# A four-layer graph network on one core: edge counts kept as 16-bit integers and widened on ScalarE

## What is computed

```python
# layer 2
neigh_mean = segment_sum(x[src], dst) / max(deg, 1)
h = x @ W_self.T + neigh_mean @ W_neigh.T + bias
x = layernorm(x + layernorm(h) * gamma + beta)
# layer 3, twice (relu between), r in {0, 1} by edge type
gate = sigmoid(x_j @ gate_w[r]);  msg = gate * x_j @ w[r]
out = segment_sum(msg, row) + x @ root + bias
```

## Time and profile before

| | us |
|---|---|
| median of 3 runs (1919.61 to 1925.85) | 1920.26 |
| the profiled execution: device time | 1923.38 |
| its span in the profile | 1921.6 |
| TensorE busy in the span | 1604.0 (83%) |
| VectorE busy | 1159.0 (60%) |
| GpSimd busy | 736.1 (38%) |
| ScalarE busy | 478.3 (25%) |

### The profile page before, as it was taken

The page is one execution under the profiler, slowest core; times in us unless marked ns, Lnnn a source line. Parts: engine busy times, 40 slices in busy tenths (PEclk is TensorE's granted clock), DMA queues, the critical chain, the costliest instruction groups (busy, mean ns, idle before and its releaser), DMA issues. The chain is left out here.

```text
span 1921.6 us, 27696 instructions
## 1 busy us (share of the span) xinstructions
PE 1604.0 (83%) x7565; PEld 978.1 (51%) x7566; DVE 1159.0 (60%) x2290; ACT 478.3 (25%) x894; POOL 736.1 (38%) x625
## 2 busy tenths in 40 slices
PE   6754975776498999998888629998499899999998
PEld 5751642334343555554455515554246545874486
DVE  5768968985455777776477776665675732122222
ACT  3301112432211555554345320000121111001200
POOL 0000887887084776661000147777661010000000
PEclk9997988999689999999989659999799999999999
DMA  0007854004901666673279327777305102430034
GB/s 25 0 20 285 280 162 121 1 1 131 345 29 60 208 202 186 187 177 68 92 281 366 129 75 209 210 209 199 85 1 156 58 1 89 150 111 1 1 137 135
DMA packets 76346, 248.96 MB, mean 130 GB/s; under 512 B 14901, under 2 KB 28582, under 8 KB 68346
## 3 DMA queue, kind: packets, MB, share of 16 engines
q1 hardware_dynamic: 38618, 147.08, 21.2%
q0 software_dynamic: 34592, 96.87, 18.9%
q10 hardware_dynamic: 3072, 4.20, 0.8%
HBM read 215.93 MB, written 32.00 MB: 129 GB/s over the span
## 5 line engine op out<-in xcount | busy, mean ns | idle before, releaser
L664 POOL DMA_INDIRECT tab_slots<-slot_words,slot_address x160 | 238.3, 1489 | 246.2 <-issue 235.5
L693 POOL DMA_INDIRECT e_rows<-tab_h,idx_h x176 | 178.9, 1017 | 292.7 <-POOLq L50 218.8
L1447 PE MATMUL dense_pY<-weights,dense_xT_block 128*128 128x512 f32 x640 | 284.2, 600 | 6.7 <-ACT dense_xT_block L1435 6.7
L1513 PE MATMUL dense_pY<-parts,dense_number 128*128 128x512 f32 x1000 | 235.5, 397 | 0.0
L994 POOL DMA_INDIRECT e_rows<-tab_q,idx_q x192 | 183.1, 954 | 98.7 <-issue 39.5
L787 PE MATMUL e_pS<-e_rows,e_onehot_ring 128*128 128x512 f32 x352 | 194.8, 644 | 21.4 <-DVE e_rows L763 19.2
L1513 PEld LDWEIGHTS dense_pY<-parts,dense_number 128*128 128x128 f32 x1000 | 187.7, 188 | 46.5 <-issue 1.4
L1447 PEld LDWEIGHTS dense_pY<-weights,dense_xT_block 128*128 128x128 f32 x640 | 120.9, 193 | 149.0 <-issue 140.4
L1067 PE MATMUL e_pS<-e_rows,e_onehot_f 128*128 128x512 f32 x384 | 181.6, 596 | 0.0
L877 PE MATMUL count_pA<-count_onehot_d,count_onehot_s 128*128 128x512 f16 (+1 forms) x576 | 116.9, 350 | 62.9 <-DVE count_onehot_d L855 59.3
L763 DVE TENSOR_TENSOR e_rows<-e_rows,e_pW 128x1024 f32<-128x1024 f32 x88 | 107.3, 1220 | 67.7 <-DMA e_rows<-tab_h,idx_h 67.6
(11 more groups left out here) (314 smaller groups left out, 2413.2 us busy)
## 6 DMA issues: line engine op xcount, KB each, us to landing
basis_piece<-in_L_gnn_basis_pieces SPq DMA_DIRECT2D x32, 2048.0 KB, 7.8
dense_number<-tab_edges_from SPq DMA_DIRECT2D x20, 1280.0 KB, 5.5
tab_edges_from<-counts_turned SPq DMA_DIRECT2D x10, 1280.0 KB
tab_edges_to<-counts_total SPq DMA_DIRECT2D x10, 640.0 KB
dense_number<-tab_edges_to SPq DMA_DIRECT2D x10, 640.0 KB, 6.0
tab_w<-basis_wout ACTq DMA_DIRECT2D x128, 32.0 KB
weights<-tab_w SPq DMA_DIRECT2D x4, 1024.0 KB, 6.6
weights<-in_L_gnn_W_T SPq DMA_DIRECT2D x3, 1024.0 KB
```

The source lines that it names most:

```text
L664: pool.indirect_dma_start(self.table, bass.IndirectOffsetOnAxis(self.address[:, t:t + 1], 0), self.words[:, t, :], None).then_inc(self.pla ...
L693: pool.indirect_dma_start(self.rows[:, q, s, :], None, self.table, bass.IndirectOffsetOnAxis(self.idx[:, j * 2 + s:j * 2 + s + 1], 0)).the ...
L1447: ins = self.nc.tensor.matmul(self.banks.at(self.bank(b, w)), self.xt[:, b % 2, c, :], weights[:, c, :], start=c == 0, stop=c == 3)
L1513: ins = self.nc.tensor.matmul(self.banks.at(self.first + b), self.number[:, self.slot(b), r * NB + k, :], self.parts[r][n][:, k, :], start ...
```

## The change

`total`, `turned` and the two tables in HBM become 16-bit unsigned integers. So each store is half as large (320 and 640 KB), and each load too; `sum2`'s loads, which take columns of `edges_to`, consist of pieces of 128 counts.

A load no longer goes to `number`. It goes to `whole`, a 16-bit view of 2560 entries per partition on the tile `wt` (edge weights, no longer needed by then). `whole` has two rooms for sum2 and one for sum3 and sum4. A new step, `widen`, is a ScalarE copy from the room to the slot of `number`, which casts to float32r. The waits are split: a load waits until its room has been widened (`widened`), a widening waits for its load and for the slot (`summed`), and TensorE's sum waits for `widened`.

SyncE's order moves: the first fetch now stands behind load 5 of sum2, the second behind load 2 of sum3. ScalarE gets 30 widenings in its written order: sum2's 0 to 3 in the last four turns of the first loop, 4 to 9 at the head of turns 1 to 6 of the second loop; for sum3 and sum4, 0 and 1 in turns 3 and 5 of the projection before, 2 to 9 in a loop beside the aggregation (for sum4 each in front of a square root of the last norm).

```diff
-        total = sb("total", [P, 2, NP], F32R)
-        turned = sb("turned", [P, 2, REL, NP], F32R)
+        total = sb("total", [P, 2, NP], U16)
+        turned = sb("turned", [P, 2, REL, NP], U16)
...
     def load(self, sp, b):
-
+        room = b % self.rooms
+        wait(sp, self.widened, self.base + b - self.rooms + 1)
+        sp.dma_start(self.whole[:, room, :, :], self.count_rows(b)).then_inc(self.loaded[room], 16)
+
+    def widen(self, act, b):
+        room = b % self.rooms
+        act.wait_ge(self.loaded[room], (b // self.rooms + 1) * 16)
         if self.base and b < 2:
-            before = 2 if self.base == NB else 1
-            wait(sp, self.summed, self.base - (1 - b) * before)
+            blocks = 2 if self.base == NB else 1
+            wait(act, self.summed, self.base - (1 - b) * blocks)
         else:
-            wait(sp, self.summed, self.base + b - self.slots + 1)
-        sp.dma_start(self.number[:, self.slot(b), :, :].bitcast(F32), self.count_rows(b)
-                     ).then_inc(self.loaded[self.slot(b)], 16)
+            wait(act, self.summed, self.base + b - self.slots + 1)
+        self.nc.scalar.copy(self.number[:, self.slot(b), :, :], self.whole[:, room, :, :]).then_inc(self.widened, 1)
 
     def sum(self, pe, b, source):
-        pe.wait_ge(self.loaded[self.slot(b)], (b // self.slots + 1) * 16)
+        pe.wait_ge(self.widened, self.base + b + 1)
...
-                if b == sum2.slots:
+                if b == sum2.slots + 2:
                     sp.wait_ge(multiplied, NB)
...
-                if b == 1:
+                if b == 2:
                     sp.wait_ge(multiplied, 2 * NB)
...
+                if n >= NB - 1:
+                    sum2.widen(act, n - (NB - 1))
 
             for n in range(NB + 1):
+                if 1 <= n <= NB - sum2.slots:
+                    sum2.widen(act, n + sum2.slots - 1)
...
-            for n, proj in enumerate((proj3, proj4)):
+            for n, (proj, agg) in enumerate(((proj3, sum3), (proj4, sum4))):
                 for b in range(NB):
-                    if b or n:
+                    if b:
                         proj.copy(act, b)
-                    if b:
                         gate(n, b - 1)
                         proj.high(act, b - 1)
+                    if b in (3, 5):
+                        agg.widen(act, b // 4)
                 gate(n, NB - 1)
                 proj.high(act, NB - 1)
-
-            for b in range(NB):
-                norm3.root(act, b, 0)
+                for b in range(NB):
+                    if b + 2 < NB:
+                        agg.widen(act, b + 2)
+                    if b == NB // 2 - 1 and n == 0:
+                        proj4.copy(act, 0)
+                    if n == 1:
+                        norm3.root(act, b, 0)
...
-    edges_to, edges_from = dram("tab_edges_to", [NP, NP]), dram("tab_edges_from", [NP, REL * NP])
+    counted = lambda n, s: nc.dram_tensor(n, s, U16, kind="Internal").ap()
+    edges_to, edges_from = counted("tab_edges_to", [NP, NP]), counted("tab_edges_from", [NP, REL * NP])
...
-                     rel_weights, gate_source, (vecs_in, 16 * (len(VECS) - 1)), out)
+                     rel_weights, gate_source, (vecs_in, 16 * (len(VECS) - 1)),
+                     flat(wt[:, :, :]).bitcast(U16)[:, 0:REL * NB * P], out)
```

More of the change, by code:

```diff
@@ L20 @@
 F32, BF16, I32 = mybir.dt.float32, mybir.dt.bfloat16, mybir.dt.int32
-F32R, F16 = mybir.dt.float32r, mybir.dt.float16
+F32R, F16, U16 = mybir.dt.float32r, mybir.dt.float16, mybir.dt.uint16
 ALU, ACT, AX = mybir.AluOpType, mybir.ActivationFunctionType, mybir.AxisListType
@@ L955, in _ @@
                 sp.wait_ge(added, b + 1)
-                sp.dma_start(both[rows, :], total[:, b % 2, :].bitcast(F32)).then_inc(stored[b % 2], 16)
+                sp.dma_start(both[rows, :], total[:, b % 2, :]).then_inc(stored[b % 2], 16)
                 sp.wait_ge(moved, (b + 1) * REL)
                 sp.wait_ge(moved_last, (b + 1) * REL)
-                sp.dma_start(by_target[rows, :], turned[:, b % 2, :, :].rearrange("p r n -> p (r n)").bitcast(F32)
+                sp.dma_start(by_target[rows, :], turned[:, b % 2, :, :].rearrange("p r n -> p (r n)")
                              ).then_inc(stored[b % 2], 16)
@@ L1480, with __init__ @@
 class Aggregation:
-    def __init__(self, nc, stage, relations, banks, number, sems, count_rows, parts):
+    def __init__(self, nc, stage, relations, banks, number, whole, sems, count_rows, parts):
         self.nc, self.base, self.relations, self.banks = nc, stage * NB, relations, banks
-        self.loaded, self.summed = sems
+        self.loaded, self.widened, self.summed = sems
         self.count_rows, self.parts = count_rows, parts
@@ L1489, in __init__ @@
         self.number = number.rearrange("p q (h k) n -> p (q h) k n", k=relations * NB)
+        self.whole = whole.rearrange("p (h k n) -> p h k n", k=relations * NB, n=P)
+        self.rooms = REL // relations
     def slot(self, b):
@@ L1519, in dense_layers @@
 def dense_layers(nc, name, C, X, acc, side, V, W, part, gate_rows, product, edges_to, edges_from,
-                 rel_weights, gate_source, vecs_in, out):
+                 rel_weights, gate_source, vecs_in, whole, out):
     held = acc
@@ L1539, in dense_layers @@
         gates_summed, gated, high_out = sem("gates_summed"), sem("gated"), sem("high_out")
-        loaded = [[sem(f"loaded{stage}_{k}") for k in range(2 * REL if stage == 0 else 2)] for stage in range(3)]
-        summed = sem("summed")
+        loaded = [[sem(f"loaded{stage}_{k}") for k in range(REL if stage == 0 else 1)] for stage in range(3)]
+        widened, summed = sem("widened"), sem("summed")
         fetched, stored = sem("fetched"), sem("stored")
@@ L1549, in aggregate @@
         def aggregate(stage, relations, rows):
-            return Aggregation(nc, stage, relations, banks, number[:, :, :, :], (loaded[stage], summed), rows, parts)
+            return Aggregation(nc, stage, relations, banks, number[:, :, :, :], whole,
+                               (loaded[stage], widened, summed), rows, parts)
         of_X, of_held = (lambda b: X[:, b, :]), (lambda b: held[:, b, :])
```

## The result

The changed kernel takes 1897.4 us (median of four runs, 1897.03 to 1900.53), the kernel before 1921.2 us in four runs of the same session. The ratio is 0.9879, 95% interval 0.9865 to 0.9893: faster by 1.2%, some 23 us. The forecast was 1898.3 in a range from 1892 to 1907. The profiled execution is the longest of the four, 1900.53 us around a span of 1898.8; the one of before took 1923.38 around 1921.6, so that pair differs by 22.9. One execution in what follows, 3207.15 us of the version with each conversion twice, lies far outside all others and is left out of that version's ratio.

A forecast was written before the change was run, and what follows sets the result against it. DMA storing 19.7 MB of counts bounds store_counts; at 2.85 us a block its last landing moves from 515.1 to 492 to 493, gaining 22 us, dense layers costing 0: 1920.3 - 22 = 1898.3 us, range 1892 to 1907.

The forecast's parts named there:

- The period of a block, 2.85 us: In store_counts: time per block with halved stores, 2.85 us in place of 5.5, from DMA and two-buffer loop with little queueing.
- (a): In store_counts: DMA limit, 2.35 us a block at 418 GB/s, 2.9 at 340 GB/s beside GpSimd's placing.
- (c): In store_counts: the engines' limit, about 2.4 us a block with TensorE at full clock.
- (b): In store_counts: two-buffer loop, block b waits for b-2's stores to land; 5.2 to 5.6 us for two blocks.
- The first landing: In store_counts: the first second-store, issued at 463.42, lands at about 466.6 in place of 468.50.
- The last store: In store_counts: block 9 issues its last store at 488.8, landed at 492 to 493; before it was 515.1.
- The dense layers at no cost: In the dense layers: 30 ScalarE conversions, 1.27 or 2.35 us each, some 60 us, all hidden; path cost 0.
- the six: Six conversions in the normalisation loop, each before a pair of roots: 1.27 us each, hidden; 8 us if cover went.
- Rival 1: In store_counts: TensorE becomes the bound at half clock, 4.0 us a block, 1905 us; 13%.
- Rival 2: In store_counts: DMA time goes by pieces, not bytes, so half the size gains little, 1918 us; 3%.
- Rival 3: In the dense layers: a conversion waiting for its load holds roots, giving back 3 to 8 us, 1901 to 1906; 7%.
- Rival 4: In the normalisation loop: late small-piece loads hold roots, VectorE and TensorE; slower than before, 1934 us at 15 us a load; 2%.

The follow-up runs named there:

- the dense part alone: Changed kernel's dense layers (16-bit loads, 30 widenings) behind the old float32 stores, against the kernel before: 1920.71 us, ratio 1.0001.
- the run with 128 bytes: Changed kernel with 8-bit counts and three rooms in the storing stage, first aggregation's loads in 128-byte pieces: 1898.12 us, ratio 0.9878 to the kernel before.

## Why the prediction was right

*What bounds the stage.* Right, and shown by halving the bytes alone.

*The period of a block, 2.85 us.* This term of the sum was too small; 3.41 was measured. The three limits were named rightly. (a) The rate of 340 GB/s beside the placing holds: 342 to 344 at a full share. (c) The engines need 2.4 us a block: TensorE's 20 transposes took 2.37 at full clock. The failing one is (b), "The loop is 5.2 to 5.6 us for two blocks". The engines' part, 2.24 us, was right (2.23 in four of the five turns, 2.56 in one). The landing, taken at 2.9 to 3.3 us from a store that ran elsewhere, took 3.87 to 5.64, 4.64 in the mean; 2.3 and 4.64 make 6.9 for two blocks, against 2 x 3.41 measured. Without the placing four landings in five took 2.97 to 3.11, as forecast: the placing, which the prediction let act on the rate alone, lengthens the landing as well. How its writes and the stores share the queues no run shows. Two blocks at 343 GB/s are 5.7 us of DMA, less than the 6.9 of the loop, so DMA stood at 0.88 to 0.94.

One of the prediction's signs of being wrong did appear: the rate fell under 300 GB/s in the stage, to 284 from 475 to 480 us, with TensorE at full clock. At its share of 0.88 that is 323 for full DMA, so it is the same error, the idle share, and not a lower rate.

*The first landing,* forecast at 466.6: block 2 started at 466.51. *The last store,* forecast to be issued at 488.8 and landed by 493: issued at 493.49, with the next stage's load at 497.54. Seven blocks at 0.56 us each above the forecast are 3.9 of the 4.7 us by which it was late; the rest is block 9, which needed 3.1 us from start to issue and not 2.24. So the stage gave 19.5 us in this pair of executions, and 19.5 to 21.5 over all of them, against 22. That the total came within 1 us of the forecast is partly luck: executions differ by some 3 us outside the stage, and that happened to lie the other way.

*The dense layers at no cost.* Right in every place: 1.25 us and 2.33 us a conversion (forecast 1.27 and 2.35 from two rows of other sizes), gaps in front of the roots, the hole, the aggregations. The weights' fetch was to start 2.9 us later, behind conversion 3: it was issued at 1437.54, which with the dense layers 22.8 us earlier is 2.5 later. The forecast held that the six would cost 8 us if their cover went; done four times over they left the loop's length alone. The gap of 2.1 to 2.6 us in front of a root is not the limit there: VectorE wants a root only in its next turn, as the prediction said, and the whole turn is cover.

*Rival 1* showed itself once. The new gaps in front of a burst were not all under 1 us, as the prediction had it, but 0.50 to 2.28. After a gap of 2.28 us a burst of 40 transposes took 6.45 us in a stretch with a granted clock of 0.66, which is half clock for part of it, and the period of that block was 3.81 us (486.58 to 490.39). From 465 to 485 us TensorE stayed at 1.00. *Rival 2* is excluded: as many pieces as before, and the stage is 19.5 us shorter. *Rival 3* is excluded by the dense part alone (1.0001).

*Rival 4 and the toll on small pieces.* The lone load in pieces of 256 bytes ran at 218 GB/s at a share of 0.95, which is 18 ns for a piece on each of 16 engines, against 27 ns for 512. The loads of counts landed in 3.2, 3.8 and 9.2 us (shortest, median, longest), against 4.2, 5.5 and 10.4. Of these the ten of the first aggregation are the ones in small pieces: 3.5 us in the median with 256 bytes, 6.0 before with 512, 2.9 in the run with 128 bytes. The rule that the fourth rival leaned on, in the Trainium skill (DMA: Bandwidth & Descriptors, Specifications), is not borne out for these loads from memory: half the piece took two thirds of the time, and not twice it.

## What to carry to other kernels

When a stage is bound by the bytes it stores, halve the bytes and then size the new limit as a loop: engine time, plus landing as it is beside all other traffic of that stage, over the number of rooms. A stage where nobody is full may be short of rooms; whether another room pays depends on what is full next (here DMA, so it won 2 us at most). A conversion on an engine in order is free as long as what stands behind it is not wanted sooner; repeating it on the chip shows how much cover there is, and where it ends. Look at who arrives last at each barrier: here GpSimd's placing ended one stage and, once the bytes were quartered, a second, and moving part of it to where that engine idled won a further 11 to 12 us, half of what this change did.

## What was not expected of the hardware

GpSimd's placing waits for some of VectorE's instructions and not for others. Of the version with the early placings, first GpSimd, then VectorE:

```profile
143.88 6.48 POOL L668 DMA_INDIRECT tab_slots<-slot_words,slot_address  x1 [0.30 <-issue]
...
166.35 1.18 POOL L668 DMA_INDIRECT tab_slots<-slot_words,slot_address  x1 [0.30 <-issue]
```

```profile
142.56 6.82 DVE L515 TENSOR_TENSOR_SCAN src_before<-src_in_bucket,src_zero 125x3200 f32<-125x3200 f32 x1
...
165.02 5.57 DVE L548 TENSOR_REDUCE src_bucket<-src_in_bucket 125x160 f32<-125x3200 f32 x1
```

The placing that met the scan ended at 150.36, 0.98 us after it; the ones that ran beside the reduction, from 166.35 on, took their 1.18 us. In the 8-bit run the placing issued beside the addition ended 1.05 us after that. The scan and the addition read two tensors, the reduction one. The Trainium skill (SBUF — State Buffer, Who interferes with whom) says that a VectorE instruction with two inputs in SBUF contends with a GpSimd instruction that reads SBUF, and that a reduction never does on this chip. These rows agree with the second, and with the first if the placing counts as one that reads SBUF: its rows name two tiles there, `slot_words` and `slot_address`.
